# First stage of each attention layer reordered, and layer b's first projections and 16 leading maximum chunks placed inside the feed-forward products

## The reference

```python
x = hidden_states                                   # (2, 1024, 256)
x = x + attn_a(layernorm(x))                        # 32 heads of 8, biases, no mask
x = x + ffn(layernorm(x))
x = x + attn_b(layernorm(x))                        # 32 query heads, 8 key/value heads, band mask
x = x + ffn(layernorm(x))

def attn(x):                                        # a; b has no biases and repeats each key head 4 times
    q, k, v = split_heads(x @ Wq + bq), split_heads(x @ Wk + bk), split_heads(x @ Wv + bv)
    scores = einsum('bhqd,bhkd->bhqk', q, k) / sqrt(8)   # b: -1e10 where i - 128 <= j < i
    return merge_heads(softmax(scores) @ v) @ Wo + bo

def ffn(x):
    h = silu(x @ w_gate) * (x @ w_up)               # (tokens, 1024)
    return keep_2_largest_of_4(h) @ w_down
```

## Time and profile before

| | us |
|---|---|
| median of 3 runs (lowest, highest) | 1824.13 (1819.83, 1828.01) |
| the profiled execution | 1828.64 |
| its span, first to last instruction | 1826.9 |
| PE busy in the span | 1703.7 (93%) |
| DVE busy | 1496.2 (82%) |
| ACT busy | 1279.9 (70%) |
| mean granted TensorE clock, share of full speed | 0.962 |

### The profile page before, as it was taken

One profiled execution on the slowest core, in us unless ns is written; L12 is line 12 of the kernel. 1 busy time (PEld: TensorE's weight loads), 2 busy tenths in 40 slices (PEclk: granted clock), 3 DMA queues, 4 the chain that ended last, 5 costly groups with the idle time before them and its releaser, 6 DMA issues.

```text
span 1826.9 us, 39166 instructions
## 1 busy us (share of the span) xinstructions
PE 1703.7 (93%) x13872; PEld 666.4 (36%) x13872; DVE 1496.2 (82%) x2150; ACT 1279.9 (70%) x2414; POOL 270.2 (15%) x613
## 2 busy tenths in 40 slices
PE   5679999999899999999976999999999999999998
PEld 3312222222222223677652222222222222247776
DVE  6599999999899992565748999999999999726564
ACT  3249999999799998322311899999999999963221
POOL 5000000000000000000011232223332233310000
PEclk9869999999999999899986899999999999989999
DMA  6833344333354311200125142222332222210000
GB/s 227 261 60 64 57 80 83 57 63 60 67 85 71 63 32 59 58 1 1 43 46 150 34 75 51 46 53 46 76 59 48 52 46 59 66 39 25 12 12 23
DMA packets 71996, 114.67 MB, mean 63 GB/s; under 512 B 12336, under 2 KB 27696, under 8 KB 71856
## 3 DMA queue, kind: packets, MB, share of 16 engines
q1 hardware_dynamic: 71856, 112.63, 28.0%
HBM read 71.96 MB, written 40.63 MB: 62 GB/s over the span
## 4 chain that ended last, share of the span: by engine, by line
PE 50%; DVE 35%; issue 10%; DMA 2%; ACT 1%; DVEq 1%; SPq 1%; POOLq 0%; ACTq 0%
DVE mneg L901 21%; PE psum L543 13%; PE psum L605 13%; DVE xn L907 10%; PE psum L525 9%; PE psum L499 5%; PE psum L623 5%; PE psum L470 2%; PE psum L583 2%; DVE mneg L907 1%; DMA k_stacks<-area 1%; PE psum L455 1%; DVEq L898 1%; PE psum L485 1%; DMA max_rows<-mT 1%
## 5 line engine op out<-in xcount | busy, mean ns | idle before, releaser
L727 ACT ACTIVATE area<-psum 128x512 f32<-128x512 f32 x2048 | 1109.0, 599 | 111.9 <-PE psum L525 88.8
L499 PE MATMUL psum<-area 64*128 64x512 bf16 x2048 | 591.5, 397 | 56.4 <-DVE mneg L907 29.2
L525 PE MATMUL psum<-area 64*128 64x512 bf16 x2048 | 638.2, 385 | 4.4 <-DMA area<-max_rows 3.6
L543 PE MATMUL psum<-area 128*32 128x256 f32 x8192 | 641.5, 391 | 0.8 <-POOL area L1092 0.4
L907 DVE CUSTOM_DVE_ANT_0 xn<-psum,band 128x1024 f32<-128x1024 f32 x512 | 591.1, 1220 | 21.6 <-PE psum L499 21.5
L901 DVE TENSOR_REDUCE mneg<-psum 128x1 f32<-128x1024 f32 x512 | 585.3, 1216 | 20.8 <-PE psum L499 20.7
L543 PEld LDWEIGHTS psum<-area 128*32 128x32 f32 x8192 | 168.9, 108 | 383.6 <-issue 243.9
L525 PEld LDWEIGHTS psum<-area 64*128 64x128 bf16 x2048 | 137.1, 94 | 456.5 <-ACT area L727 409.4
L768 ACT ACTIVATE area<-psum 128x512 f32<-128x512 f32 x64 | 38.2, 597 | 181.6 <-PE psum L605 181.5
L499 PEld LDWEIGHTS psum<-area 64*128 64x128 bf16 x2048 | 106.4, 94 | 110.0 <-DVE mneg L907 54.6
L935 DVE TENSOR_TENSOR area<-psum,area 128x512 f32<-128x512 f32 x64 | 44.0, 690 | 118.9 <-PE psum L605 112.1
(11 more groups left out here) (67 smaller groups left out, 760.8 us busy)
## 6 DMA issues: line engine op xcount, KB each, us to landing
ctx_rows<-area SPq DMA_DIRECT2D x64, 256.0 KB, 2.1
area<-q_stacks SPq DMA_DIRECT2D x32, 384.0 KB, 7.9
area<-k_stacks SPq DMA_DIRECT2D x64, 192.0 KB, 6.4
area<-q_stacks_b SPq DMA_DIRECT2D x32, 384.0 KB, 6.1
area<-q_stacks SPq DMA_DIRECT2D x32, 192.0 KB, 3.8
area<-q_stacks_b SPq DMA_DIRECT2D x32, 192.0 KB, 3.2
area<-ctx_rows SPq DMA_DIRECT2D x16, 256.0 KB, 4.4
area<-inv_rows SPq DMA_DIRECT2D x16, 256.0 KB, 5.2
```

Source lines behind the costliest of these rows:

```text
L499: mm = pe.matmul(psum[:, 2 + 2 * (c % 2) + half, :], q_max[lo:lo + PAR, buf, head, tile * P:(tile + 1) * P], k_max[lo:lo + PAR, buf, 0 if ...
L525: pe.matmul(psum[:, S_BANKS[slot % len(S_BANKS)], :], k_st[lo:lo + PAR, buf, 0 if a else head // 2, kt * P:(kt + 1) * P], q_st[lo:lo + PAR ...
L543: mm = pe.matmul(psum[head * VW:(head + 1) * VW, PV_BANK, cols], vaug[:, buf, kt, head, :], probs[:, u % PRING, head, cols], start=(kt == ...
L727: act.activation(probs[:, u % PRING, head, :], psum[:, S_BANKS[slot_of(u, head, ahead) % len(S_BANKS)], :], ACT.Exp, scale=SCALE).then_inc ...
```

## The change

Four things are moved, in the hand-written lists of all five engines.

1. **Start of layer a.** The first batch element is projected and split (`split(0, 0)`) before the second one's transposes. The second batch element's projections, split steps and values (`project_half(0, 1, i)`, `split_step`, `copy_v`) stand between the leading chunks: one projection half at each even chunk 0 to 14, one tile pair of values at chunks 9, 11, 13 and 15. The second half of x is loaded behind the first two weights. The second batch element's projections use two PSUM banks instead of four (`behind`).
2. **POOL's clearing.** Matmuls now read exactly the 48 rows (maxima) or 51 rows (scores) that hold data, and the three maximum rows move from row 56 to row 48. So of each layer's clearings two of 4096 columns go, one shrinks from 4096 to 2048, and one of 2048 stays. The clearings of layer a stand first on POOL, the building of the band mask behind group 0, and the addition of the output bias to x (L1132 before, L1243 after) behind the first `split_max`. Layer b's k stack for the maxima has a tile of its own (`k_max_b`), so that it can be loaded during the feed-forward block.
3. **Start of layer b.** `norm(2, 0)`, `project(1, 0)` and `split(1, 0)` move ahead of `gate_up(3, 0)`. Leading chunks 0 to 15 stand inside `down(2)`, `gate_up(3, 1)` and `down(3)`, all in one pair of PSUM banks (6 and 7), each one waiting for the one before it to be reduced. Chunks 16 to 31 follow with `project_half(1, 1, i)` at chunks 16, 18, ... 26 and the values at 27.
4. **End of the second feed-forward block.** `down(2)` moves behind `gate_up(3, 1)`.

The core of the diff, by engine:

```diff
@@ tables
+        V_CHUNKS = [(9, 11, 13, 15), (27,)]
+        P_CHUNKS = [range(0, CPH, 2), range(CPH, CPH + 12, 2)]
+        def max_bank(a, g, c):
+            return 6 if in_feed(a, g, c) else 2 + 2 * (c % 2)
-        SLOT = [0, 1, 2, 3, 0, 1, 2, 3] + [0, 1, 0, 2, 3, 1]
+        SLOT = [0, 1, 2, 3, 0, 1, 2, 3] + [4, 5, 4, 6, 7, 8]
@@ sync
             for a in range(2):
                 store_stacks(a, 0)
+                if a == 1:
+                    stored_all(a, 1)
+                sp.wait_ge(ones_set, a + 1)
+                load_st_stack(a, 0, 0)
+                if a == 1:
+                    move_max(a, 0, 0, 0)
                 store_stacks(a, 1)
...
-                load_st_stack(a, 0, 0)
-                move_max(a, 0, 0, 0)
+                if a == 0:
+                    move_max(a, 0, 0, 0)
+                stored_all(a, BATCH)
@@ tensor
+            def project_half(a, b, i):
...
+                behind = 2 if b == 1 else 4
+                if n >= behind:
+                    pe.wait_ge(rest_done, n - behind + 1)
...
-                    pe.wait_ge(max_used, n - 1)
+                    pe.wait_ge(max_used, n if in_feed(a, g, c) else n - 1)
                 for half in (1, 0):
                     lo = PAR * half
-                    mm = pe.matmul(psum[:, 2 + 2 * (c % 2) + half, :],
-                                   q_max[lo:lo + PAR, buf, head, tile * P:(tile + 1) * P],
-                                   k_max[lo:lo + PAR, buf, 0 if a else head, :], start=True, stop=True)
+                    mm = pe.matmul(psum[:, max_bank(a, g, c) + half, :],
+                                   q_max[lo:lo + ROWS, buf, head, tile * P:(tile + 1) * P],
+                                   k_max_b[lo:lo + ROWS, buf, :] if a else k_max[lo:lo + ROWS, buf, head, :],
+                                   start=True, stop=True)
...
+                for c in range(CPH * a, CHUNKS):
+                    if c in P_CHUNKS[a]:
+                        project_half(a, 1, P_CHUNKS[a].index(c))
+                    if c in V_CHUNKS[a]:
+                        project_v(a, 1, V_CHUNKS[a].index(c))
...
+                    max_scores(a, 0, 0, c)
...
                 gate_up(a, 2, 1)
-                gate_up(a, 3, 0)
-                down(a, 2)
                 if a == 0:
                     norm_transpose(2, 0)
                     project(1, 0)
-                gate_up(a, 3, 1)
-                down(a, 3, last=INNER // P // 2 - 1)
-                down(a, 3, first=INNER // P // 2)
-                if a == 0:
+                    gate_up(a, 3, 0)
+                    down(a, 2, leading=range(0, 4))
+                    gate_up(a, 3, 1, leading=range(4, 8))
+                    down(a, 3, last=INNER // P // 2 - 1, leading=range(8, 12))
+                    down(a, 3, first=INNER // P // 2, leading=range(12, 16))
                     norm_transpose(2, 1)
-                    project(1, 1)
+                else:
+                    gate_up(a, 3, 0)
+                    gate_up(a, 3, 1)
+                    down(a, 2)
+                    down(a, 3, last=INNER // P // 2 - 1)
+                    down(a, 3, first=INNER // P // 2)
@@ scalar
+            norm(0, 0)
+            copy_transposed(0, 0)
+            norm(0, 1)
             act.wait_ge(bias_loaded, 64)
+            split(0, 0)
+            copy_transposed(0, 1)
+            split(0, 1)
@@ vector
             def attend(a):
-                for c in range(CHUNKS):
+                for c in range(CPH * a, CHUNKS):
                     maxima(a, 0, c)
+                    if c in P_CHUNKS[a] or c - 2 in P_CHUNKS[a]:
+                        split_step(a, 1, (c - P_CHUNKS[a][0]) // 2)
+                    if c - 1 in V_CHUNKS[a]:
+                        copy_v(a, 1, V_CHUNKS[a].index(c - 1))
...
+                    measure(2, 0)
+                    gated_product(a, 2, 1, 0)
+                    scale(2, 0)
+                    hidden(a, 2, 1, begun=1)
                     split(1, 0)
+                    hidden(a, 3, 0, leading=range(0, 4))
+                    add_down(a, 2)
+                    hidden(a, 3, 1, between=range(4, 8), leading=range(8, 12))
+                    add_down(a, 3, leading=range(12, 16))
                     norm(2, 1)
@@ gpsimd
-                pool.memset(area[:, q_max_at:q_max_end], 0.0)
...
-                pool.memset(area[:, ones_at:vaug_at], TWO_ONES[a]).then_inc(area_set, 1)
-                pool.memset(area[:, vaug_at:q_st_at], 1.0)
+                pool.memset(area[:, k_st_at:vaug_at], TWO_ONES[a]).then_inc(ones_set, 1)
+                pool.memset(area[:, vaug_at:q_st_at], 1.0).then_inc(vaug_set, 1)
...
-                pool.memset(area[:, q_st_at:q_max_at], 0.0).then_inc(area_set, 1)
-                extend_v(a, 0, 0)
-                split_max(a, 0, 0)
+                extend_v(a, 0, 0)
+                if a == 0:
+                    split_max(a, 0, 0)
```

More of the change, by code:

```diff
@@ L48 @@
 ROWS = HD * BLOCKS
-MROW = ROWS + 8
 PAR = 64
@@ L607, in gate_up, with down @@
                         mm.then_inc(done, 1)
-            def down(f, c, first=0, last=INNER // P - 1):
+                    if leading:
+                        max_scores(1, 0, 0, leading[r])
+            def down(f, c, first=0, last=INNER // P - 1, leading=()):
                 half = INNER // P // 2
                 pe.wait_ge(sparse_done, 8 * f + 2 * c + last // half + 1)
-                if f == 0 and c == 3 and first == 0:
+                if f == 0 and c == 2 and first == 0:
                     pe.wait_ge(v_done, VBASE[1] + VCH[1])
@@ L755, in group @@
                         copy_turned(a, g + 1, 0)
+                    if first and a == 1 and u == 2:
+                        stacks_out(a)
                     exps(a, g, u, ahead)
@@ L888, in split @@
-                copy_v(a, b)
+                    split_step(a, b, i)
+                for v in range(VCH[a]):
+                    copy_v(a, b, v)
             def maxima(a, g, c):
@@ L942, in hidden @@
                     gated_product(f, c, h, r)
+                    if between:
+                        maxima(1, 0, between[r])
                 dve.wait_ge(mag_done, 4 * (n0 + 1))
@@ L953, in hidden @@
                     gated_product(f, *follower, 0)
+                if leading:
+                    maxima(1, 0, leading[0])
                 if n0:
@@ L999, in _ @@
             dve.wait_ge(bias_loaded, 64)
-            for b in range(BATCH):
-                split(0, b)
+            split(0, 0)
             for a in range(2):
```

333 lines of the change are left out of this document (188 added, 145 removed).

## The result

The changed kernel takes 1791.76 us (median of 4 runs, 1791.55 to 1792.12), the kernel before took 1823.25 beside it: ratio 0.9826, 95% interval 0.9803 to 0.9848. Forecast were 1790 and a range of 1779 to 1809. The profiled execution took 1791.92 us, its span is 1790.2, TensorE is busy 95% of it and VectorE 83%, the mean granted clock is 0.975.

The account below looks back on a forecast made before the run. The chain of waits was led by VectorE's maximum reductions, with matmuls sharing most of the rest. Gains of 20 (layer a), 9.5 (layer b) and 5 (end), 34.5 us in all, gave 1790 us from 1824.1; range 1779 to 1809.

Parts of the forecast that it names:

- the second gate: Layer a's start: ACT's copy of turned maxima waits until the last stack lands at 88.6; first score at 95.6.
- VectorE's floor: Layer a's chunks: VectorE's reductions, split steps and value copies take 50.2 us from 44.4, so not before 94.6.
- VectorE paces layer a's groups from the first: Layer a's groups: a start d us earlier should end the layer d us earlier.
- low after that: Expected sign in layer a's start: clock above 0.8 from 45 to 80 us, then low.
- Saving and growth: Layer b: 22.2 us saved from last norm to first score, feed-forward block 12.7 us longer; gain 9.5.
- the terms 3.6, 5.7 and 1: Feed-forward block: eight chunks where TensorE bounds 3.6 us, chunks in `down(3)` 5.7, 64-row matmul pairs between full-array products 1.
- The term for the wait on the reused buffer and the table: Feed-forward block: ACT's table reload by `norm(2, 0)` 0.6 us, wait for the reused part buffer 1.8.
- A: Leading stages: TensorE stays at 1.2 GHz between chunks; 1816 for the whole stage, 1803 for half; chance 0.14.
- B: Layer b: chunks inside the feed-forward block cost what they save, gain 0: 1799; chance 0.10.
- C: Layer a: POOL's bias addition starts before the last low part, last store 8 us late: 1798; chance 0.05.
- D: All chunks: the two matmuls covering 48 rows no longer run side by side: about 1995; chance 0.02.
- E: First scores: stack loads and stores queue; 8 us gained in layer a, 0 in layer b: 1811; chance 0.05.

Follow-up runs that it names:

- the kernel without them: Changed kernel plus matmuls with unread results from the gap behind chunk 16 and in the first groups, ACT's exponential table loaded early: 1785.79 us, ratio 0.9788.
- the profile in which the clock was back earlier: Changed kernel with the 16 chunks inside the feed-forward block computed by full-array bf16 matmuls from constants: one run, 1789.05 us.
- four kernels with fillers: Changed kernel plus 128x128x128 float32 matmuls, results never read, at four sets of places in TensorE's idle time: 1799.32, 1802.38, 1793.17 and 1785.79 us.

## Why the prediction was right

**The sum** held: 34.5 forecast, 36.7 measured between the profiles. Some of that is luck: errors of the terms cancel in both layers.

**Layer a.** The way to the first chunk was right to 0.6 us (44.4 and 43.82; with the late clock it is near 46), with the scaling as priced and confirmed by the clearings put back. The gain at the first score was sized too low, 20 against 24.9. The step that failed is the second gate, "88.6, and 7 us": I carried the 11 us of the old last store over, and it landed within 5.4 us of its issue (76.04 to the copy at 81.44), so that VectorE's floor set the mark alone. That floor was put at 94.6, of which the 1.7 us that I took off in layer b should have gone as well, and the 2 us for TensorE's order and a round-up came on top.

**What I left out** took part of it back. "VectorE paces layer a's groups from the first" is not so when TensorE enters the group at 1.2 GHz with scores, maxima and products with v to do: 3.65 us of holes in place of 0.5, shown by the kernel without them and by the profile in which the clock was back earlier. I had seen "low after that" for the clock, and priced only the chunks with it. The two errors are 4.9 and -3.0 us and largely cancel: 21.9 us in place of 20, partly by luck.

**Layer b.** Saving and growth are each 1.0 us above the forecast, so their difference, 9.5, is right by luck. Inside the growth the chunks took 10.2, where the terms 3.6, 5.7 and 1 make 10.3, but the single prices differ: 0.5 to 0.65 us each where TensorE is the bound, not 0.45, and the two waits in `down(3)` are 2.29 and 1.58 us (forecast 2 to 4 each). The term for the wait on the reused buffer and the table was 2.4 and measured 3.5: TensorE's wait went from 1.52 to 4.11 us. A change of tile shape was priced at 0.1 us and comes to about 0.15. The longer holes of layer b's first group don't show against the kernel before: with the end undone the stretch behind its first score is 815.7 us, as before.

**The end**: 5 forecast, 5.2 by the kernel that undoes it alone.

**Rivals.** A was right for chunks 17 to 31, where the engine stood half empty, and wrong for the rest; its price came due one stage later. B is refuted by 7.8 us. C was real, and avoided because L969 started 0.74 us first. D falls by the rows: in layer a's groups (130 to 700 us) the chunk matmuls with 48 rows took 383 ns on the mean in the changed kernel, and those with 64 rows 383 before. E did not show: the last store had landed at 81.44, 10 us before the first score, and the first reduction waited for no transfer.

## What to carry to other kernels

Price a half-empty stretch by the stage behind it too: here the low clock cost nothing among the chunks and about 4 us in each layer's first group. Of the four kernels with fillers only the one whose fillers began in the first hole and reached to where real work fills the engine gained; begun one chunk later they cost 6 us. And where two engines hold each other up, ask which instruction starts first, and how much of a long one is left when the other comes: the same pair cost 0, 2 and 8.3 us, by the start alone.

## What the runs showed of the hardware

- TensorE, filled only from behind a hole of 1.85 us, lost its upper clock 1 us later, was busy 29.3 of 30 us from 77 to 107 and stood at 1.2 GHz in both rows of that stretch (0.52 and 0.50); filled from that hole on, it was busy 12.2 of 14 us and kept 2.4 GHz.
- A subtraction of VectorE with two SBUF operands is held to the end of a POOL addition (8.96 us in place of 0.68), while those with a PSUM operand and the reductions beside it kept 0.74 and 1.13 us. The scaling by per-partition scalars, with one SBUF operand, is held by POOL's clearings (7.92 in place of 2.67). A short POOL instruction that starts behind VectorE's subtraction is held to its end in turn (0.54 in place of 0.22).
- A chunk whose matmuls use 48 rows, placed between full-array products at full clock, costs 0.3 us more than one of full-array matmuls with the same columns: an estimate of 0.15 us for each change of tile shape.
- In 8 of 13 executions the first projections took 1.7 to 2.5 us longer: their first three to five products ran at 1.06 us and more in place of 0.59, and the first clock record of 1.00 begins behind them, at 19.5 to 20.9 us (25.5 with the clearings put back), where it begins at 14.2 to 15.5, ahead of them, in the other five. What decides between the two is open.
